# Expert steps on one core: transposes of the activations ahead of the down products, low halves ahead of the gating of results

## What is computed

```python
def step(y, ew):                      # once for each of 16 experts
    wg, wu, wd, c = ew
    h = silu(xf @ wg.T) * (xf @ wu.T)             # 176 wide
    return (y + h @ wd.T * c[:, None], None)
y, _ = lax.scan(step, y0, (Wg, Wu, Wd, coeff.T))
z = silu(xf @ Sg.T) * (xf @ Su.T) @ Sd.T          # shared expert, 352 wide
x = x + gb * (y + z)
```

## Time and profile before

| | us |
|---|---|
| time, median of 3 runs | 569.58 |
| lowest and highest of them | 567.87 and 569.83 |
| the profiled execution, first to last instruction (its span) | 566.3 |
| PE busy in the span | 492.5 (87%) |
| DVE busy | 396.3 (70%) |
| POOL busy | 291.9 (52%) |
| ACT busy | 284.1 (50%) |

### The profile page before, as it was taken

One profiled execution on the slowest core, in us unless ns is written; L12 is line 12 of the kernel. 1 busy time (PEld: TensorE's weight loads), 2 busy tenths in 40 slices (PEclk: granted clock), 3 DMA queues, 4 the chain that ended last, 5 costly groups with the idle time before them and its releaser, 6 DMA issues. The chain is left out here.

```text
span 566.3 us, 12354 instructions
## 1 busy us (share of the span) xinstructions
PE 492.5 (87%) x3575; PEld 464.1 (82%) x3575; DVE 396.3 (70%) x1099; ACT 284.1 (50%) x743; POOL 291.9 (52%) x330
## 2 busy tenths in 40 slices
PE   2699999999999999998430488999999999999996
PEld 0589998999999898988330377999999999999995
DVE  6769953456867768687763798867777776784575
ACT  2368754554554545533262564555655655553331
POOL 6446603010346446465766799544444444446994
PEclk9999999999999999999555599999999999999999
DMA  7457996779747456422858443343434444356951
GB/s 196 134 170 217 254 307 205 196 206 229 209 125 216 139 164 183 124 86 83 267 203 271 135 132 103 116 136 119 140 120 127 132 124 137 119 158 249 413 204 74
DMA packets 62982, 98.00 MB, mean 173 GB/s; under 512 B 9747, under 2 KB 48210, under 8 KB 61574
## 3 DMA queue, kind: packets, MB, share of 16 engines
q1 hardware_dynamic: 50664, 57.80, 37.8%
q0 software_dynamic: 9136, 32.53, 15.2%
q10 hardware_dynamic: 3118, 6.89, 3.9%
HBM read 60.49 MB, written 40.04 MB: 178 GB/s over the span
## 5 line engine op out<-in xcount | busy, mean ns | idle before, releaser
L1702 POOL DMA_INDIRECT ys_scr<-h,ids_st x59 | 61.0, 1033 | 67.4 <-DVE h L1756 63.9
L140 POOL DMA_INDIRECT xs_scr<-h,slot_u x64 | 62.9, 982 | 54.0 <-PE TB L1302 26.6
L105 PE MATMUL GU<-gu_hi,xT 128*128 x316 | 84.1, 348 | 1.9 <-DVE xT L1736 1.9
L1626 ACT ACTIVATE aT<-HT 88x256 fp32r<-88x256 f32 (+1 forms) x95 | 37.8, 399 | 65.9 <-PE HT L1862 65.9
L105 PE MATMUL YP<-dn_hi,aT 88*128 x316 | 67.1, 304 | 4.4 <-DVE aT L1741 3.9
L1748 DVE TENSOR_TENSOR h_act<-GU,g_act 128x176 f32<-128x176 f32 (+1 forms) x95 | 35.2, 371 | 46.4 <-ACT g_act L1619 46.2
L919 ACT ACTIVATE prob<-TB 128x512 f32<-128x512 f32 x64 | 38.2, 597 | 56.5 <-PE TB L1302 55.8
L1312 PE MATMUL O<-raw,prob 128*128 128x99 f32 x512 | 66.2, 275 | 0.0
L1312 PEld LDWEIGHTS O<-raw,prob 128*128 128x128 f32 x512 | 61.6, 192 | 0.1
L105 PEld LDWEIGHTS YP<-dn_hi,aT 88*128 88x128 f32 x316 | 47.5, 188 | 11.1 <-issue 7.5
L105 PEld LDWEIGHTS GU<-gu_hi,xT 128*128 128x128 f32 x316 | 52.1, 192 | 2.3 <-issue 2.3
(11 more groups left out here) (243 smaller groups left out, 1252.8 us busy)
## 6 DMA issues: line engine op xcount, KB each, us to landing
x_st<-xs_scr SPq DMA_DIRECT2D x79, 144.0 KB
dn_hi<-k_scr SPq DMA_DIRECT2D x48, 192.0 KB, 3.8
planes<-ys_scr POOLq DMA_DIRECT2D x8, 1024.0 KB, 17.1
k_scr<-raw SPq DMA_DIRECT2D x8, 768.0 KB, 6.1
dn_hi<-q_scr SPq DMA_DIRECT2D x24, 256.0 KB, 4.4
q_scr<-raw SPq DMA_DIRECT2D x8, 512.0 KB, 3.6
raw<-in_egu SPq DMA_DIRECT2D x8, 352.0 KB
raw<-in_x SPq DMA_DIRECT2D x16, 128.0 KB, 4.0
```

The costliest lines, as they stand in the source:

```text
L105: mm = eng.matmul(out, a, b, start=(i + j == 0), stop=(i == len(pairs) - 1 and j == 2))
L140: eng.indirect_dma_start(T["xs_scr"], bass.IndirectOffsetOnAxis(ap=T["slot_u"][:, par, t % 2, k:k + 1], axis=0), T["h2"][:, row, :], None) ...
L1626: eng.activation(aT[0:rows, p2, 0, 0:k, :], HT[p2][0:rows, 0:k * P].rearrange("p (k x) -> p k x", k=k), ACT.Copy).then_inc(aT_hi, 1)
L1702: eng.indirect_dma_start(ys, bass.IndirectOffsetOnAxis(ap=ids_st[:, r:r + 1].bitcast(U32), axis=0), results(r % 8), None).then_inc(sent[q] ...
```

## The change

Two pairs of neighbours swap places, in each expert step and in each shared tile. On PE, the transposes of the activations of the step before (`transpose_a(s-1)`) go ahead of the down products of the step before that (`down(s-2)`). On DVE, the low half of those activations (`a_lo(s-1)`) goes ahead of the scaling of the results (`y_gate(s-2)`; in shared tiles `keep_late` and `add_late`). At the end of the shared tiles the down products of tile 14 now come between the transposes of tiles 14 and 15. No instruction is added or removed; ACT, POOL and SP have the same order as before.

```diff
@@ VectorE, expert step
             x_lo(s + 2, p2)
+            if runs(s, 1):
+                a_lo(s - 1, 1 - p2, FH, 2)
             if runs(s, 2):
                 y_gate(s - 2, (r - 2) % UNROLL, i if r % 4 >= 2 else i - 1)
-            if runs(s, 1):
-                a_lo(s - 1, 1 - p2, FH, 2)
@@ VectorE, shared tile
                 x_lo(NS + n + 2, p2)
+            if n == 0:
+                a_lo(NS - 1, 1 - p2, FH, 2)
+            else:
+                a_lo(NS + n - 1, 1 - p2, P, SH_K)
             if n < 2:
                 s = NS + n - 2
                 y_gate(s, s % UNROLL, s // 4)
...
-            if n == 0:
-                a_lo(NS - 1, 1 - p2, FH, 2)
-            else:
-                a_lo(NS + n - 1, 1 - p2, P, SH_K)
@@ TensorE, expert step
             transpose_x(w + 2, (t + 2) % 4, i + (2 if t >= 2 else 1))
+            if runs(s, 1):
+                transpose_a(w - 1, 1 - p2, FH, 2)
             if isinstance(s, int) and 2 <= s < NE + 2:
                 eng.wait_ge(dn_lo, s - 1)
             if runs(s, 2):
                 down(w - 2, p2, before)
-            if runs(s, 1):
-                transpose_a(w - 1, 1 - p2, FH, 2)
@@ TensorE, shared tile and end
                 transpose_x(w + 2, (w + 2) % 4, (w + 2) // 4 + 1)
+            if n == 0:
+                transpose_a(w - 1, 1 - p2, FH, 2)
+            else:
+                transpose_a(w - 1, 1 - p2, P, SH_K)
             if n < 2:
                 down(w - 2, p2, load_entry(w - 2))
             else:
                 shared_down(w - 2, p2)
...
+        shared_down(NS + TILES - 2, 1 - p2)
         transpose_a(NS + TILES - 1, p2, P, SH_K)
-        for w in (NS + TILES - 2, NS + TILES - 1):
-            shared_down(w, w % 2)
+        shared_down(NS + TILES - 1, p2)
```

## The result

| | before | after |
|---|---|---|
| time, median of 6 runs each, us | 569.21 | 561.51 |
| lowest and highest | 567.87 to 572.66 | 557.97 to 568.16 |
| the profiled execution's span | 566.3 | 560.3 |

By the medians that is 7.7 us less. The ratio, which is of the fast runs alone (all but the one of 568.16), is 0.9845 with a 95% interval of 0.9803 to 0.9886: 8.8 us less, between 6.5 and 11.2. The forecast was 559.2, 10.4 us less, with a range of 555.5 to 565.5. So it was right in direction, and some 2 us too hopeful. This part says where the two spans differ; the later ones say why.

The account below looks back on a forecast made before the run. A closed loop from transposes through ACT and DVE to the down products was taken to set the steady pitch, with PE only just keeping up. Gains 5.8 + 0.9 + 3.3 + 0.4 = 10.4 took 569.6 to 559.2 us, range 555.5 to 565.5.

Parts of the forecast that it names:

- Steady steps: Steps 19 to 78: opening the loop brings the pitch from 2.207 to near 2.10 us, 5.8 us gained, at most 6.3.
- The closed loop through HT, ACT, VectorE and YP: Steady steps: transposes, ACT's copy, VectorE's low half and down products wait on each other, 2.20 us from HT to HT.
- The two rivals that priced the setting of addresses: Gap ahead of YP is address setting, time 565.4, chance 0.10; or setting is uncovered at GU, time 579.3, chance 0.07.
- Steps 12 to 19: Same loop at pitch 2.30; 1.4 us possible against 2.10, cut to 0.9 for VectorE's low halves of weights.
- Steps 0 to 12: Step 7's weight half on VectorE starts earlier, between POOL's two, and takes 0.88 us; 3.3 us gained, between 0.4 and 4.4.
- The last tile: End of the shared tiles: the last products start at about 561.1 instead of 561.48; 0.4 us gained, between nothing and 1.0.
- Shared tiles, "Nothing": Shared tiles: PE is full and the same work stands between gating and next GU in another order, so no gain.
- nobody waits for it within four steps: POOL waits for the later scaling of results, but is busy under half of the time; priced at nothing.
- The 3.3 that were added to make a time of it: The runs' median lies 3.3 us above the profiled span, so a span of 555.9 becomes a time of 559.2.

Follow-up runs that it names:

- pe_only: The change's order on TensorE with the old order on VectorE; median 566.29 us, ratio to before 0.9931.
- dve_only: The change's order on VectorE with the old order on TensorE; median 573.08 us, ratio to before 1.0068.
- early_only: The new order of TensorE and VectorE in steps 0 to 18 alone, everything behind as before; median 565.02 us, ratio 0.9916.
- steps_only: The new order in the 79 expert steps alone, shared tiles and end as before; median 561.57 us.
- sp_adds: The changed kernel with POOL's three loads of `to_add` moved to SyncE's queue; median 562.43 us.
- light: The changed kernel with POOL's third sum of tiles 12 to 15 given to VectorE; median 561.75 us.
- before_light: The kernel before with POOL's third sum of tiles 12 to 15 given to VectorE; median 570.47 us, ratio 1.0015.
- best1: light with VectorE's first pair of planes added one tile later and the last tile's transposes and low half ahead of the last but one's products; median 562.52 us.
- best3: The changed kernel with earlier plane loads, five third sums on VectorE, last tile's transposes ahead, old order in tiles 0 and 1; median 559.46 us, ratio 0.9816.

## Why the prediction was right, and where it was not

- **Steady steps, right.** Forecast 5.8, measured 5.61, pitch 2.112. The closed loop through HT, ACT, VectorE and YP set the pace, though PE was shown as busy all the time, and pe_only opens it by TensorE's order alone; the sum of PE's own starts, 2.10, is what came. The two rivals that priced the setting of addresses fall: no gap stands ahead of YP or GU.
- **Steps 12 to 19, right but small.** 0.9 forecast, 1.30 measured, nearly the whole 1.4 that I had cut for VectorE's weight halves. They held nothing back: the halves for the steps 13 to 15 end 0.35 to 0.37 us ahead of their GU before and 0.36 to 0.52 after. In pe_only they end only 0.16 to 0.17 ahead, and the seven steps still take 14.75.
- **Steps 0 to 12, right.** 3.3 forecast, 3.26 measured, by the mechanism named: step 7's half in POOL's gap. Up to GU of step 8 the gain is 0.58; the rest comes in the four steps behind it. In five kernels (before, after, pe_only, dve_only and early_only) I compared the nine halves that VectorE makes from 10 us after the first gate_up on. The 19 that met at most 0.12 us of POOL's took 0.88. The other 26 took 1.67 to 2.45 and ended 0.75 to 0.76 after POOL's. The Trainium skill (SBUF — State Buffer, section "SBUF: two separate sides") says that the two engines hold their shared ports as a lock for a whole instruction, whoever starts first. In 23 of the 26 VectorE's half starts behind POOL's, and these rows agree. In the other three it starts 0.04 to 0.39 us ahead of POOL's by the profile and still ends behind it, which "first" alone doesn't explain. Against the prediction's reading of its rows, where two of three such halves end with POOL's: its rows hold two of them, and in the trace both end 0.76 after POOL's.
- **The last tile, right and of no use.** 0.4 forecast, 0.42 measured, and not in the time, since the end wasn't the last tile's.
- **Shared tiles, "Nothing": this step failed.** I looked at PE alone there, as in the earlier trace rows, and said of POOL that nobody waits for it within four steps. That holds in the steady steps. Behind the last one POOL's own chain begins: last scatter, loads, 36 sums, and a closing that outlasts the last store. The same swap that gains in the steps delays this chain's start by 1.87, and the sums then took 0.47 more (60.69 for 58.35). These 2.34 are what is missing between the 10.17 gained up to step 78 and the 7.83 that arrived. The wait for the planes, 0.56, was missed too, but cost nothing at the end.
- **The end of the sum.** The chain of waits in the earlier trace rows ends with the last addition at 563.26, and the sum left the 3 us behind it as they were, without asking what ends them. That the span ended 8.00 after POOL's last sum could have been read from POOL's timeline before.
- **The time, closer than the span, by luck.** The span was forecast at 555.9 and came at 560.3: 2.6 of the 4.4 are missing from the first gate_up on, 1.8 lie in the stretch ahead of it. The 3.3 that were added to make a time of it were too much: a run's time lies 1.8 above its own span (562.12 for 560.3), and the rest was the difference between runs. So the time was missed by 2.3 only.

## What to carry to other kernels

An engine that is full by its busy time can still run in a loop with others: compare the starts of its instructions with the end of what each waits for, and add up its own work, to see whether an order opens the loop. A swap that pays in a loop's body can cost at its exit, where the last results start another engine's chain; look there separately, and ask of every engine how long after its last work the program may end. And two swaps can be worth little alone and much together, when the one only moves the wait to where the other stands.

## What the runs showed of the hardware

- POOL's program closes 7.74 to 7.77 us after its last work in thirteen of the fourteen kernels, whatever ran last, and 7.52 after it in sp_adds; the span ends 8.0 after that work where nothing else is later. What POOL does in that time isn't settled. Where the stores end the program (early_only, steps_only, sp_adds, light, before_light, best1, best3), they do so 2.9 us after the start of the last addition.
- One of VectorE's low halves in after began 0.39 us ahead of POOL's, while POOL was still at a scatter, and yet ended 0.76 after POOL's, 2.45 long: starting first wasn't enough there.
